# Macaron layer (mixture-of-experts FFN, attention, FFN): the shared expert's up values and the affinities in one product, its down product on stacked high and low parts

## The reference

```python
x = x + 0.5 * ffn(layernorm(x))
x = x + attention(layernorm(x))
x = x + 0.5 * ffn(layernorm(x))

def ffn(xf):                                    # D = 128, F = 64, E = 64 experts, top 8
    shared = silu(xf @ Ws_up) @ Ws_down         # (T, D) @ (D, F), then @ (F, D)
    aff = xf @ centroids.T                      # (T, E)
    _, idx = top_k(aff + expert_biases, 8)
    w = sigmoid(take_along_axis(aff, idx)); w = w / sum(w)
    cw = zeros(T, E).at[tokens, idx].add(w)
    h = silu(einsum('td,edf->etf', xf, W_up))   # every expert for every token
    y = einsum('etf,efd->etd', h, W_down)
    return shared + einsum('etd,te->td', y, cw)
```

## Time and profile before

| | |
|---|---|
| median of 3 runs | 580.72 us (580.37 to 582.02) |
| profiled execution: time, span | 581.23 us, 579.4 us |
| PE busy | 553.9 us (96%), 2737 instructions |
| DVE busy | 434.2 us (75%), 911 instructions |
| ACT busy | 408.5 us (71%), 808 instructions |
| POOL busy | 279.8 us (48%), 250 instructions |
| mean granted clock of PE | 0.981 |
| passes 0 to 3, attention, passes 4 to 7 | about 0 to 238, 238 to 377, 377 to 579 us |

### The profile page before, as it was taken

One profiled execution on the slowest core, in us unless ns is written; L12 is line 12 of the kernel. 1 busy time (PEld: TensorE's weight loads), 2 busy tenths in 40 slices (PEclk: granted clock), 3 DMA queues, 4 the chain that ended last, 5 costly groups with the idle time before them and its releaser, 6 DMA issues.

```text
span 579.4 us, 8712 instructions
## 1 busy us (share of the span) xinstructions
PE 553.9 (96%) x2737; PEld 447.1 (77%) x2737; DVE 434.2 (75%) x911; ACT 408.5 (71%) x808; POOL 279.8 (48%) x250
## 2 busy tenths in 40 slices
PE   7889999899989999989999999899999999999997
PEld 5567777677867777669999999778777777877885
DVE  4478669977995686677777988698868968875664
ACT  5758776687758777476666666677776777687774
POOL 5668774766675566200000000055764766566663
PEclk9589999999989999999999999999999999999999
DMA  6448564454545544000000000045564564566653
GB/s 203 138 130 212 170 202 148 130 172 166 169 138 165 186 151 164 1 1 1 2 1 1 1 2 1 1 123 176 171 199 146 165 193 152 170 173 196 182 188 98
DMA packets 46734, 72.22 MB, mean 125 GB/s; under 512 B 8720, under 2 KB 12816, under 8 KB 46688
## 3 DMA queue, kind: packets, MB, share of 16 engines
q1 hardware_dynamic: 45984, 71.14, 39.9%
q0 software_dynamic: 160, 0.26, 0.3%
q10 hardware_dynamic: 544, 0.26, 0.2%
HBM read 69.53 MB, written 2.10 MB: 124 GB/s over the span
## 4 chain that ended last, share of the span: by engine, by line
PE 75%; DVE 11%; POOL 5%; ACT 4%; issue 3%; DMA 1%; SPq 0%; POOLq 0%; DVEq 0%; ACTq 0%
PE lrow L964 11%; PE lrow L965 11%; PE lrow L966 11%; PE bank L1006 9%; PE bank L1008 8%; PE bank L1007 8%; PE bank L1012 5%; PE bank L1204 3%; PE bank L1206 3%; PE bank L1205 3%; POOL gpart_lo L252 2%; DVE gated L624 2%; DVE rs L649 2%; DMA raw<-in_w_up 1%; DVE rs L647 1%
## 5 line engine op out<-in xcount | busy, mean ns | idle before, releaser
L252 POOL TENSOR_TENSOR gpart_lo<-gated,gpart_hi 128x512 fp32r<-128x512 f32 x174 | 223.9, 1293 | 192.8 <-ACT gpart_hi L418 188.8
L407 ACT ACTIVATE lrow<-lrow 128x512 f32<-128x512 f32 (+1 forms) x252 | 147.3, 585 | 62.8 <-PE lrow L966 62.0
L624 DVE TENSOR_TENSOR gated<-lrow,wide 128x512 f32<-128x512 f32 x166 | 114.0, 687 | 48.5 <-ACT lrow L407 44.9
L418 ACT CAST gpart_hi<-gated 128x512 fp32r<-128x512 f32 x174 | 106.5, 613 | 7.3 <-DVE gated L624 6.8
L1006 PE MATMUL bank<-gpart_lo,wdn_hi 128*128 128x512 f32 x256 | 103.0, 402 | 2.9 <-POOL gpart_lo L252 2.7
L1008 PE MATMUL bank<-gpart_hi,wdn_hi 128*128 128x512 f32 x256 | 102.0, 399 | 0.0
L1007 PE MATMUL bank<-gpart_hi,wdn_lo 128*128 128x512 f32 x256 | 101.5, 397 | 0.0
L624 DVE TENSOR_TENSOR lrow<-lrow,wide 128x512 f32<-128x512 f32 x78 | 54.1, 694 | 29.8 <-ACT lrow L407 29.6
L418 ACT CAST gpart_hi<-lrow 128x512 fp32r<-128x512 f32 (+1 forms) x90 | 53.2, 591 | 31.0 <-DVE lrow L624 30.7
L252 DVE TENSOR_TENSOR gpart_lo<-lrow,gpart_hi 128x512 fp32r<-128x512 f32 (+1 forms) x90 | 61.4, 683 | 5.6 <-ACT gpart_hi L418 4.9
L899 DVE TENSOR_TENSOR pT_lo<-bank,pT_hi 128x512 fp32r<-128x512 f32 x64 | 43.7, 684 | 25.7 <-ACT pT_hi L568 25.7
(11 more groups left out here) (212 smaller groups left out, 1004.7 us busy)
## 6 DMA issues: line engine op xcount, KB each, us to landing
wide<-gates_dram SPq DMA_DIRECT2D x488, 128.0 KB, 3.0
raw<-in_w_up SPq DMA_DIRECT2D x8, 256.0 KB, 4.5
raw<-in_w_down SPq DMA_DIRECT2D x8, 256.0 KB, 5.8
gates_dram<-gates SPq DMA_DIRECT2D x8, 128.0 KB, 2.2
x<-in_x SPq DMA_DIRECT2D x3, 256.0 KB, 3.4
out_dram<-x SPq DMA_DIRECT2D x3, 256.0 KB, 3.2
x<-in_x ACTq DMA_DIRECT2D x1, 128.0 KB, 2.7
x<-in_x SPq DMA_DIRECT2D x1, 128.0 KB, 2.5
```

Of the source, the lines that this page charges most:

```text
L252: return eng.tensor_tensor(gpart[1][0:m, U % NGP, :], gated_at(U)[0:m, :], gpart[0][0:m, U % NGP, :].bitcast(F32), ALU.subtract)
L407: nc.scalar.activation(dst[0:m, :], hid[U % NH][0:m, :], ACT.Silu).then_inc(s_silu, 1)
L418: nc.scalar.copy(gpart[0][0:m, U % NGP, :], gated_at(U)[0:m, :]).then_inc(s_ghi, 1)
L624: nc.vector.tensor_tensor(gated_at(U), a, b, ALU.mult).then_inc(s_gated, 1)
```

## The change

Unit 0 is taken out of every pass but n = 0 and n = 4 (`for u in range(min(c, 1), UNITS)`; `place(u, n)` now numbers the units). For the other six passes:

- `joint_product(n)` at u = 11 of the pass ahead, in the place of `pro_aff`: one product of 3 matmuls of 512 columns, with centroids and `Ws_up` side by side as the weights, into bank `mq`. Rows 0 to 63 are the affinities (turned: experts on the partitions), rows 64 to 127 the shared expert's up values. It waits for `e_x` too, since `mq` was last read by DVE's `epi_x`.
- `joint_aff` (ACT, u = 12) copies rows 0 to 63 out, `joint_turn` (PE, u = 13) turns them back with four transposes of 64 columns, and DVE reads them from `mp` as before.
- `joint_silu` (ACT, u = 13), `joint_hi` (ACT, u = 14) and `joint_lo` (DVE, u = 14) put the low part in rows 0 to 63 and the high part in rows 64 to 127 of one tile `shared`.
- `joint_down(n)` at u = 4 of the pass itself, in the place of `down(0)`: 2 matmuls over 128 rows. The first has the weights' low part in rows 64 to 127 under zeros (`wsdn_pad`), the second the high part twice (`wsdn`).
- The routing steps behind it come one u later: on DVE `pro_aff` 13 and 14, `pro_top` 15, 16, 18, `pro_sum` 21; on POOL `weights` 19, `normed_weights` 22; on ACT `pro_sil` 16, `pro_cwT` 26; on PE `pro_cw` 25; on SP `STORE = 31`.
- At the start, `Ws_down` is loaded a second time into rows 64 to 127 (POOL's queue, behind the biases), and POOL, ACT and DVE prepare `wsdn_pad` and `wsdn`.

```diff
-STORE = 30
+STORE = 31
...
+            nc.gpsimd.dma_start(rawd[F:P, :], wsdn_d).then_inc(s_value, 16)
...
-                            if u == 18:
+                            if u == 19:
                                 weights(n + 1)
-                            if u == 21:
+                            if u == 22:
                                 normed_weights(n + 1)
...
+            def joint_aff(n):
+
+                act.wait_ge(j_out, joint(n))
+                nc.scalar.copy(affT[:, :], mq[0:E, :]).then_inc(j_aff, 1)
+
+            def joint_silu(n):
+
+                nc.scalar.activation(mq[E:P, :], mq[E:P, :], ACT.Silu).then_inc(j_silu, 1)
+
+            def joint_hi(n):
+
+                act.wait_ge(j_silu, joint(n))
+                nc.scalar.copy(shared[E:P, :], mq[E:P, :]).then_inc(j_hi, 1)
...
-                            act.wait_ge(s_value, 16 * 2)
+                            act.wait_ge(s_value, 16 * 3)
...
+            def joint_lo(n):
+
+                dve.wait_ge(j_hi, joint(n))
+                nc.vector.tensor_tensor(shared[0:F, :], mq[F:P, :], shared[F:P, :].bitcast(F32), ALU.subtract).then_inc(j_lo, 1)
...
+            def joint_product(n):
+
+                pe.wait_ge(p_lo, n + 1)
+                if n % NCH > 1:
+                    pe.wait_ge(e_x, n - 1)
+                else:
+                    pe.wait_ge(s_gated, (n - 1) * PAIRS + EARLY)
+                product(mq[:, :], [s[:, 0:E + F] for s in small], [a[:, n % 2, :] for a in xnT[n // NCH]]).then_inc(j_out, 1)
+
+            def joint_turn(n):
+
+                pe.wait_ge(j_aff, joint(n))
+                for i in range(TPC):
+                    ins = nc.tensor.transpose(mp[:, i * E:(i + 1) * E], affT[:, i * P:(i + 1) * P], ident[0:E, 0:E])
+                ins.then_inc(p_aff, 1)
+
+            def joint_down(n):
...
+                pe.wait_ge(j_lo, joint(n))
+                y = yacc[n % 2][:, :]
+                nc.tensor.matmul(y, wsdn_pad[:, :], shared[:, :], start=True, stop=False)
+                nc.tensor.matmul(y, wsdn[0][:, :], shared[:, :], start=False, stop=False)
...
-                    for u in range(UNITS):
+                    for u in range(min(c, 1), UNITS):
...
                             if u == 11:
-                                pro_aff(n + 1)
-                            if u == 24:
+                                joint_product(n + 1)
+                            if u == 13:
+                                joint_turn(n + 1)
+                            if u == 25:
                                 pro_cw(n + 1)
```

More of the change, by code:

```diff
@@ L154, in macaron_kernel @@
         s_eps, s_zero = sem("eps_made"), sem("cw_zeroed")
+        j_out, j_aff, j_silu, j_hi, j_lo = (sem("shared_" + n) for n in ("and_aff", "aff_copied", "silu", "hi", "lo"))
+        s_pad = sem("wsdn_pad_zeroed")
         f_xT, f_hi, f_lo, f_bias = (sem("first_" + n) for n in ("xT", "hi", "lo", "biased"))
@@ L223, in slot_of, with place, unit_at, before @@
             return (nth_gated(u, n) - 1) % NB
+        def place(u, n):
+            return n * PAIRS + u + n // NCH
+        def unit_at(U):
+            f, at = divmod(U, NCH * PAIRS + 1)
+            return ((at - 1) % PAIRS + 1, f * NCH + (at - 1) // PAIRS) if at else (0, f * NCH)
+        def before(u, n):
+            return unit_at(place(u, n) - 1)
+        def joint(n):
+            return n - n // NCH
         def on_pool(U):
-            n, u = divmod(U, UNITS)
+            u, n = unit_at(U)
             return u % 3 != 0 and (u < UNITS - 1 or n % NCH < NCH - 1)
@@ L248, in low_part @@
         def low_part(eng, U):
-            m = P if U % UNITS else F
+            m = P if unit_at(U)[0] else F
             eng.wait_ge(s_ghi, U + 1)
@@ L520, in _ @@
                         if c or u > 1 - f:
-                            hi_unit(*((u - 1, n) if u else (UNITS - 1, n - 1)))
+                            hi_unit(*before(u, n))
                         if c + 1 < NCH:
@@ L626, in lo_unit @@
             def lo_unit(u, n):
-                if not on_pool(n * UNITS + u):
-                    low_part(nc.vector, n * UNITS + u).then_inc(s_glo, 1)
+                if not on_pool(place(u, n)):
+                    low_part(nc.vector, place(u, n)).then_inc(s_glo, 1)
             def raw_stats(k, c, tiles):
@@ L824, in _ @@
                             lo_unit(0, n)
-                    for u in range(UNITS):
+                            pad_lo()
+                    for u in range(min(c, 1), UNITS):
                         gate_unit(u, n)
                         if c or u > 1 - f:
-                            lo_unit(*((u - 1, n) if u else (UNITS - 1, n - 1)))
+                            lo_unit(*before(u, n))
                         if c + 1 < NCH:
-                            if u == 0:
+                            if u == min(c, 1):
                                 if f == 0:
@@ L995, in down @@
                     pe.wait_ge(s_w, 2 * ((u - 1) // (PAIRS // WP)) + 2)
-                if u == 0 and n == 1:
-                    pe.wait_ge(w_Alo, 1)
-                if u == 0 and n % NCH >= 2:
-                    pe.wait_ge(e_y, n - 1)
                 if U == 0:
@@ L1132, in _ @@
                             spread_gate(u, n)
-                        if u >= LAG:
+                        if u > LAG or u == LAG and c == 0:
                             down(u - LAG, n)
                         elif c:
-                            down(UNITS - LAG + u, n - 1)
+                            down(PAIRS - LAG + u, n - 1)
+                            if u == LAG:
+                                joint_down(n)
                         if c + 1 < NCH:
```

67 lines of the change are left out of this document (44 added, 23 removed).

## The result

| | before | after |
|---|---|---|
| median (runs) | 580.93 us (578.99 to 582.61, 6) | **584.81 us** (583.61 to 585.34, 6) |
| ratio to before | | **1.0068**, 95% interval 1.0049 to 1.0087 |
| profiled execution: time, span | 581.23 us, 579.4 us | 585.14 us, 583.3 us |
| PE busy | 553.9 us, 2737 instructions | 547.5 us, 2683 instructions |
| PE idle (span less busy) | 25.5 us | 35.8 us |

What follows compares the result with a forecast made beforehand. PE was taken to bound the kernel, with three quarters of the chain. 581.23 less 7.9 (heads) plus 10.8 (middles) gave 584.1 for the profiled execution, which lies 0.5 above the median: 583.7 us, range 576.5 to 589.

Steps and rivals of the forecast that it cites:

- Sign and mechanism: Slower by 0.5%: POOL's `weights` comes late, so DVE's `pro_sum` waits and PE's `up(25)` starts late; slower had 0.56.
- the decisive step: On POOL, `weights` comes only behind unit 19's low part, so `p_w` is ready at 511.65 and `pro_sum` stands 1.8 us.
- The head: Start of six passes: PE loses `up(0)` and `down(0)`, gains `joint_down`; 1.31 us less each, 7.9 us in all.
- The turn: `joint_turn` on PE in the middle of a pass: 0.6 us taken, bounds 0.44 and 0.82.
- The chain in pass 5: Hand-over from `p_top` through `weights` and `pro_sum` to PE: `up(25)` at 514.45 instead of 512.9, `up(26)` at 516.9 to 517.0.
- The middle: Routing stretch inside six passes: loses 10.8 us in sum, bounds 6 to 15.
- Passes 4 to 6: Their middles are alike and lose 2.0 us each, 6.0 in all.
- Pass 0: Its middle, where POOL also splits the weights: a PE stall of 0.86 goes, the rest comes; loses 1.0 us.
- ACT's three operations: The three operations added to ACT, busy 71% of the span: costed at nothing; without cover each costs 0.6 us.
- Passes 1 and 2: Middles with attention's preparation: the stall for `xn` shrinks by some 1, is given back at `up(22)`; lose 1.9 us each.
- PE's busy time: In the changed profile: PE's busy time 8 us down or so, its idle time up by 10.
- the clock: Pass 2's fall, 1 us lost at least, left out of the sum; rival: falls in two or more middles, 587 to 592, 0.14.

Runs made afterwards that it cites:

- b_no_unit0: The kernel before without unit 0 in six passes, the shared expert's share missing in the output there; 569.38 us, ratio 0.9809.
- The better version: Changed kernel with POOL's `weights` back at u = 18, `value_parts` at u = 23, and `joint_lo` at u = 23 in passes 0, 4, 5, 6; 570.15 us.
- a_weights20: The changed kernel with POOL's `weights` behind the low part of unit 20 instead of 19, nothing else; 590.64 us, ratio 1.0176.
- b_value23: The kernel before with attention's value parts on POOL (passes 1 to 3) at u = 23 instead of 18; 580.41 us, ratio 0.9991.

## Why the prediction was right, and where it was off

- **Sign and mechanism: right.** Forecast 583.7, measured 584.81. `pro_sum` waits six times, 12.2 us in total (forecast some 10). Taking back the decisive step alone gave 8.2 us, and putting it alone into the kernel before cost 9.2 (580.51 to 589.74).
- **The head, −1.31 a pass: right.** Unit 0 costs 1.79 (b_no_unit0). Timeline of PE, pass 1 of the changed kernel, `joint_down` between two ordinary products:

```profile
83.92 0.39 PE L1086 MATMUL bank<-shared,wsdn_pad 128*128 128x512 f32 x1
84.15 0.40 PE L1087 MATMUL bank<-shared,wsdn_hi 128*128 128x512 f32 x1
84.39 0.39 PE L1019 MATMUL lrow<-xnT_lo_a,wup_hi 128*128 128x512 f32 x1
```

  It takes 0.47, as worked out.
- **The turn, 0.6 between bounds of 0.44 and 0.82: 0.58.** From the last start ahead of it to the second behind it, less two ordinary starts (1.05 less 0.47), timeline of PE, pass 5:

```profile
499.69 0.40 PE L1059 MATMUL bank<-gpart_hi,wdn_hi 128*128 128x512 f32 x1
500.02 0.46 PE L1074 MATMUL bank<-ident,affT 64*128 64x64 f32 x4
500.41 0.50 PE L1019 MATMUL lrow<-xnT_lo_b,wup_hi 128*128 128x512 f32 x1
500.74 0.39 PE L1020 MATMUL lrow<-xnT_hi_b,wup_lo 128*128 128x512 f32 x1
```

  So of the 0.38 that the matmuls over 64 rows cost more in the earlier trace rows, the turn pays 0.14 at most, against the 0.44 of `pro_cw`.

- **The chain in pass 5.** On the old axis (less 3.05): `p_top` 507.74 (forecast 507.45), `weights` done 511.89 (511.65), wait of the sum 1.71 (1.8), `up(25)` 514.64 (514.45), `up(26)` 517.01 (516.9 to 517.0). The middle lost 2.11 (2.0). It misses one stall, PE's 0.42 at 516.23 ahead of `down(20)`, whose low part comes late with `weights` ahead of it; it lies inside the time that `up(25)` would have waited anyway.
- **Passes 4 to 6.** With a head of −1.31 the three distances give middles of 2.1, 2.2 and 2.2, forecast 2.0 each.
- **Pass 0, forecast 1.0: mis-sized.** It measured 1.18 + 1.31 = 2.5, at the same clock as before (0.97). I had counted POOL's load and left out that ACT and DVE also prepare weights there. PE's timeline in pass 0 of the changed kernel:

```profile
45.38 0.46 PE L1074 MATMUL bank<-ident,affT 64*128 64x64 f32 x4 [0.41 <-ACT affT L450]
...
50.81 0.33 PE L1019 MATMUL bank<-qT_lo,qT_hi 128*128 128x128 f32 x1 [1.98 <-DVE qT_lo L826]
```

  And in the kernel before, where nothing stood in the place of the first:

```profile
50.02 0.33 PE L964 MATMUL bank<-qT_lo,qT_hi 128*128 128x128 f32 x1 [1.36 <-DVE qT_lo L778]
```

  DVE's timeline of the changed kernel shows what stands ahead of `qT_lo` (50.33):

```profile
49.61 0.69 DVE L713 TENSOR_TENSOR shared<-bank,shared 64x512 fp32r<-64x512 f32 x1 [0.63 <-ACT shared L459]
```

  Two steps of the prediction failed here. ACT's three operations were costed at nothing, but DVE stands 0.63 for one of them, `joint_hi` (L459). And the 0.61 of `joint_lo` was laid into DVE's list of pass 5 alone; pass 0 was taken from POOL's rows, without what waits behind `joint_lo` there. Moving only `joint_lo` away gave 1.42 back in this pass, with PE's wait for `qT_lo` down from 1.98 to 0.53; taking away all of the shared expert's rest gave 2.54, of which `joint_down` is 0.47.
- **Passes 1 and 2, forecast 1.9 each:** pass 1 gives 0.80 + 1.31 = 2.1. The working behind it was off: the stall for `xn`, which was to shrink by some 1, went whole, and four others came (0.47 at 112.54, 0.57 at 114.08, 0.86 at 118.71, 0.33 at 122.71). In pass 2 the clock of the earlier trace rows did not fall. The changed kernel's window, columns as there:

```profile
166.00:168.00 2.00, 1.53 (x7) 0.77 (x5) 1.97 (x11) 1.38 (x3) 1.99 (x2) 1.00 0.42 149
```

  I had left this out of the sum as open; by the starts behind the stall in the kernel before (eight steps from 165.37 to 168.84, 3.47 us, 1.87 at the ordinary pace) it is worth 1.6. From pass 2's mark to the end of the first FFN the changed kernel took 0.26 less; so without that gift the middle there would be −0.26 + 1.31 + 1.6 = 2.65.
- **PE's busy time:** forecast 8 us down, idle 10 up; 6.4 down, 10.3 up. The 6.4 aren't the work that went: a slowed stretch counts as busy for longer, and up to pass 0's mark, where the clock was 0.81 before and is 0.90 after, busy time already fell by 2.4 (27.11 to 24.68).

The errors have both signs (1.5 too little in pass 0, 0.2 in pass 1, 0.75 in pass 2, 0.4 in passes 4 to 6, 1.6 too much for the clock, 0.25 at the start), so that 584.1 for the profiled execution stands beside 585.14 is partly luck.

One point changes the forecast little and the advice much: I put nearly the whole loss of the middle on the order. The runs split it. Against 573.0 (580.93 less the head's 7.9) the changed kernel loses 11.8 us, 8.2 of them by the place of `weights`. The added work measured 4.8 and 5.0 where it was taken away. That is 1.2 to 1.4 more than the 3.6 that are left; against it stand gains that the 573.0 leaves out, above all the stalls for `xn` of the earlier trace rows. The better version ends below 573; that it owes this to the same stalls is argued and not shown.

What stays open: how the 5.0 us of volume divide between ACT and DVE, in passes 1 and 2 above all, and what `joint_lo` at u = 23 is worth in the better version.

## What to carry to other kernels

When a step on a slow, in-order engine is moved by one place in a hand-written list, price what it is moved behind: not the 1.3 us that this instruction takes, but the time at which its own input arrives; an idle engine with a ready instruction behind one that isn't is the row to look for. Work taken off the bounding engine pays only after the chain that releases its next operands is laid out again: the same product was 0.7% slower in the order that it came with, and 1.8% faster with three steps put elsewhere. And an operation "hidden" on an engine that is busy 71% must be laid into that engine's timeline at the place where it comes.

## What the runs showed of the hardware

- An operation of DVE can stand while POOL runs one. The four-element L805 takes 0.17 us alone and 0.78 beside POOL's low part, ending 0.03 behind it (516.21 against 516.18). The kernel before shows it too (its L757 took 0.73 at 509.69, beside the first of POOL's low parts from 509.10). In a_weights20, where POOL is idle at that place, it took 0.17 in every pass. In the changed kernel the one-input reduction ahead of it began 0.08 behind the start of the same low part and was not held (0.42). The two-input comparison L746 ended 0.28 behind POOL's low part of unit 17 (510.79; low part from 509.21 for 1.30), as before the change. The Trainium skill, SBUF — State Buffer, "SBUF: two separate sides", says that DVE and POOL share one pair of ports, locked for a whole instruction, and that DVE wants it for two inputs in SBUF or in a two-port mode. The comparison and the reduction agree with that; whether L805 ran in such a mode, no run here shows.
- A clock fall is not tied to a stall's length. In the kernel before, PE stood 1.36 us in pass 1 and kept a granted clock of 1.00, and stood 1.38 in pass 2 and got 0.50 behind it, the 1.2 GHz level. In b_value23 the stall in pass 1 is the same 1.36 (at 109.89), and there the clock fell. The windows behind it, the kernel before first, columns as in the earlier trace rows:

```profile
112.00:114.00 2.00, 1.78 (x8) 1.14 (x7) 1.93 (x4) 2.00 (x5) 1.92 (x4) 1.00 0.19 72
...
112.00:114.00 2.00, 2.00 (x6) 1.18 (x5) 1.97 (x4) 2.00 (x5) 1.15 (x1) 0.50 0.53 145
```

- A mean clock doesn't tell the time. The changed kernel stands longer in all and is slower, and its mean clock is higher, 0.990 against 0.981. Much of the kernel before's low clock lies ahead of pass 0's mark (0.81 up to there, 0.90 in the changed kernel), and yet it reaches that mark only 0.25 us later (35.16 against 34.91).
